# A routing stage with one-hot tiles formed sixteen columns ahead instead of four

## The reference

```python
logits = xf @ gate_w.T                         # 8192 tokens, 8 experts
rw, sel = jax.lax.top_k(logits, 2)
rw = jax.nn.softmax(rw)
for e in range(8):
    we = jnp.sum(jnp.where(sel == e, rw, 0.0), axis=-1)
    h = jax.nn.silu(xf @ w1[e].T) * (xf @ w3[e].T)
    out = out + h @ w2[e].T * we[:, None]
```

## Time and profile before

| | us |
|---|---|
| median of 3 runs (3143.37, 3150.48, 3153.46) | 3150.48 |
| the profiled execution | 3142.74 |
| its span, first to last instruction | 3141.0 |
| routing stage, first DVE operation to last | 2303.93 to 2394.75 |
| expert stage, first instruction to the end | 2396.20 to 3141.0 |

### The profile page before, as it was taken

One profiled execution on the slowest core, in us unless ns is written; L12 is line 12 of the kernel. 1 busy time (PEld: TensorE's weight loads), 2 busy tenths in 40 slices (PEclk: granted clock), 3 DMA queues, 4 the chain that ended last, 5 costly groups with the idle time before them and its releaser, 6 DMA issues. The chain is left out here.

```text
span 3141.0 us, 63979 instructions
## 1 busy us (share of the span) xinstructions
PE 2903.5 (92%) x22889; PEld 1810.8 (58%) x22890; DVE 2306.6 (73%) x4073; ACT 1885.7 (60%) x3422; POOL 655.7 (21%) x940
## 2 busy tenths in 40 slices
PE   5888988886699999999999999998978999999998
PEld 4666766675233333333333333336766888888886
DVE  5776667664799999999999999976876444444443
ACT  3556555652288888888888888883333333333332
POOL 1222122211000000000000000001101555555554
PEclk8889998997699999999999999998879999999999
DMA  1223332332222222222222222216932333333332
GB/s 38 104 91 114 113 115 78 114 113 93 71 87 70 74 80 71 70 68 67 68 65 68 70 71 70 71 42 217 297 123 69 50 50 50 49 49 50 50 49 42
DMA packets 179210, 259.29 MB, mean 83 GB/s; under 512 B 31208, under 2 KB 118528, under 8 KB 179024
## 3 DMA queue, kind: packets, MB, share of 16 engines
q1 hardware_dynamic: 130432, 187.48, 19.2%
q0 software_dynamic: 31152, 52.33, 8.6%
q10 hardware_dynamic: 17440, 16.98, 1.7%
HBM read 134.92 MB, written 119.60 MB: 81 GB/s over the span
## 5 line engine op out<-in xcount | busy, mean ns | idle before, releaser
L868 DVE TENSOR_REDUCE b_mxq<-b_p_m 128x1 f32<-128x1024 f32 x1024 | 1221.9, 1221 | 70.6 <-PE b_p_m L891 63.2
L792 ACT ACTIVATE b_probs<-b_p_e 128x512 f32<-128x512 f32 x2048 | 1105.6, 597 | 147.5 <-PE b_p_e L939 38.7
L891 PE MATMUL b_p_m<-b_kst,b_qst 64*128 64x512 f32 x2048 | 765.0, 454 | 27.7 <-DMA b_vst<-v_d 23.5
L939 PE MATMUL b_p_e<-b_qst,b_kst 64*128 64x512 f32 x2048 | 747.1, 444 | 0.4 <-ACT b_probs L792 0.4
L910 PE MATMUL b_p_o<-b_probs,b_vst 128*32 128x256 f32 x8208 | 642.1, 390 | 0.5 <-ACT b_probs L792 0.4
L939 PEld LDWEIGHTS b_p_e<-b_qst,b_kst 64*128 64x128 f32 x2048 | 315.6, 184 | 419.4 <-ACT b_probs L792 355.0
L1668 ACT ACTIVATE d_act<-d_p_up 128x512 f32<-128x512 f32 x136 | 81.3, 598 | 491.2 <-PE d_p_up L1741 491.2
L910 PEld LDWEIGHTS b_p_o<-b_probs,b_vst 128*32 128x32 f32 x8208 | 168.2, 108 | 324.2 <-issue 187.5
L891 PEld LDWEIGHTS b_p_m<-b_kst,b_qst 64*128 64x128 f32 x2048 | 319.7, 187 | 58.8 <-DVE b_mxq L868 30.9
L1637 POOL DMA_INDIRECT out_dram<-d_y,d_to x136 | 217.7, 1601 | 217.7 <-DVE d_y L1702 205.0
L1756 PE MATMUL d_p_y<-w2T,d_hT 128*128 x1096 | 259.1, 379 | 0.8 <-ACT d_hT L1662 0.8
(11 more groups left out here) (308 smaller groups left out, 4057.7 us busy)
## 6 DMA issues: line engine op xcount, KB each, us to landing
b_qst<-qk_d SPq DMA_DIRECT2D x384, 64.0 KB
b_kst<-qk_d SPq DMA_DIRECT2D x384, 64.0 KB
x1y_d<-a_x1y SPq DMA_DIRECT2D x32, 512.0 KB, 4.4
qk_d<-a_hi SPq DMA_DIRECT2D x32, 512.0 KB, 2.8
qk_d<-a_lo SPq DMA_DIRECT2D x32, 512.0 KB, 3.7
v_d<-a_v_s SPq DMA_DIRECT2D x16, 1024.0 KB, 6.9
b_vst<-v_d SPq DMA_DIRECT2D x64, 256.0 KB
c_xy<-x1y_d SPq DMA_DIRECT2D x16, 1024.0 KB, 8.6
```

Source lines behind the costliest of these rows:

```text
L792: nc.scalar.activation(probs[(2 * step + e % 4 // 2) % BUFS][:, (e % 2) * 512:(e % 2 + 1) * 512], p_e[(slot(e) if more1 else e) % EB][:], ...
L868: V_.reduce_max(mxq[half][:, h, qt:qt + 1], p_m[j % 2][:], AX.X).then_inc(s["m_red"], 1)
L891: mm(p_m[j % 2][:, kh * 512:(kh + 1) * 512], qst[r][rows(h), qt * P:(qt + 1) * P], kst[r][rows(h), kh * 512:(kh + 1) * 512], start=True, s ...
L939: mm(p_e[u % EB][:], kst[r][rows(h), kt * P:(kt + 1) * P], qst[r][rows(h), a * 512:(a + 1) * 512], start=True, stop=True).then_inc(s["e_ps ...
```

## The change

The ring gets 16 places. `is_lo` and `is_hi` become slices of two large tiles, `lo_tiles` and `hi_tiles`, and the integer tables of the prelude (`iota_i`, `val_i`, `slot_i`, `of_i`, `hi_i`, `lo_i`) and `first` are put into places 8 to 15 of them, which the columns reach only after the prelude is done with its tables. `own`, `end_of` and `past` are computed at the end of the prelude, PE multiplies `p_ex` before the columns of expert 0, `experts_of_tiles` moves from e = 2 to e = 1, and the semaphore `rank_ps` goes: one wait on `ex_ps` covers both products.

```diff
+    RING = 16
+    lo_tiles, hi_tiles = sb("lo_tiles", [P, RING, P]), sb("hi_tiles", [P, RING, WIDE])
+    is_lo, is_hi = [lo_tiles[:, r] for r in range(RING)], [hi_tiles[:, r, 0:TILES] for r in range(RING)]
+    spare = [hi_tiles[:, r].bitcast(i32) for r in range(8, 14)]
+    iota_i, iota = spare[0], sb("iota", [P, WIDE])
...
+    first, first_sum = lo_tiles[:, 8:16].rearrange("p r (c e) -> p (r c) e", e=NE), sb("first_sum", [P, C2])
-    RING = 4
-    is_lo = [sb(f"is_lo{r}", [P, P]) for r in range(RING)]
-    is_hi = [sb(f"is_hi{r}", [P, TILES]) for r in range(RING)]
...
         V_.tensor_scalar(other[:], chose[:], -1.0, 1.0, ALU.mult, ALU.add).then_inc(s["other_done"], 1)
+        then(V_.tensor_tensor(own[:], end[:], ident[:, 0:NE], ALU.mult))
+        then(V_.reduce_sum(end_of[:], own[:], AX.X))
+        V_.tensor_scalar(past[:], iota[:, 0:TILES], end_of[:, 0:1], None, ALU.is_ge).then_inc(s["past_done"], 1)
...
-            dve.wait_ge(s["rank_ps"], 1)
+            dve.wait_ge(s["ex_ps"], 1)
...
-            then(V_.tensor_tensor(own[:], end[:], ident[:, 0:NE], ALU.mult))
-            then(V_.reduce_sum(end_of[:], own[:], AX.X))
-            V_.tensor_scalar(past[:], iota[:, 0:TILES], end_of[:, 0:1], None, ALU.is_ge).then_inc(s["past_done"], 1)
...
             if e == 1:
                 ranks()
-            if e == 2:
                 experts_of_tiles()
...
             if e == 0:
                 pe.wait_ge(s["other_done"], 1)
                 mm(p_rank, lower_r[:], other[:], start=True, stop=False, skip_group_check=True)
-                mm(p_rank[:, 1], ones_r[:], other[:, 0], start=False, stop=True, skip_group_check=True).then_inc(s["rank_ps"], 1)
-            if e == 1:
+                mm(p_rank[:, 1], ones_r[:], other[:, 0], start=False, stop=True, skip_group_check=True)
                 pe.wait_ge(s["past_done"], 1)
                 mm(p_ex, ones_b[:], past[0:NE, :], start=True, stop=True).then_inc(s["ex_ps"], 1)
```

More of the change, by code:

```diff
@@ L1356, in invert_places_and_transpose_weights @@
     WIDE = max(P, TILES)
-    iota_i, iota = sb("iota_i", [P, WIDE], i32), sb("iota", [P, WIDE])
+    RING = 16
[3 more added lines that the diff above has]
+    iota_i, iota = spare[0], sb("iota", [P, WIDE])
     lanes_i, early_i, early = sb("lanes_i", [P, TILES], i32), sb("early_i", [P, 2], i32), sb("early", [P, 2])
@@ L1366, in invert_places_and_transpose_weights @@
     valid, empty_i, inv_i, choice_i, before_i = sb("valid", [P, TILES]), sb("empty_i", [P, TILES], i32), sb("inv_i", [P, TILES], i32), sb("choice_i", [P, TILES], i32), sb("before_i", [P, TILES], i32)
-    val_i, val = sb("val_i", [P, C2], i32), sb("val", [P, C2])
+    val_i, val = spare[1][:, 0:C2], sb("val", [P, C2])
     base_i, base = sb("base_i", [P, NE], i32), sb("base", [P, NE])
     total, full, full_i, tiles, end, begin = sb("total", [P, NE]), sb("full", [P, NE]), sb("full_i", [P, NE], i32), sb("tiles", [P, NE]), sb("end", [P, NE]), sb("begin", [P, NE])
-    slot_i, of_i, of, hi_i, lo_i, hi, lo = sb("slot_i", [P, C2], i32), sb("of_i", [P, C2], i32), sb("of", [P, C2]), sb("hi_i", [P, C2], i32), sb("lo_i", [P, C2], i32), sb("hi", [P, C2]), sb("lo", [P, C2])
-    first, first_sum = sb("first", [P, C2, NE]), sb("first_sum", [P, C2])
-    RING = 4
-    is_lo = [sb(f"is_lo{r}", [P, P]) for r in range(RING)]
-    is_hi = [sb(f"is_hi{r}", [P, TILES]) for r in range(RING)]
+    slot_i, of_i, hi_i, lo_i = (spare[r][:, 0:C2] for r in range(2, 6))
+    of, hi, lo = sb("of", [P, C2]), sb("hi", [P, C2]), sb("lo", [P, C2])
+    first, first_sum = lo_tiles[:, 8:16].rearrange("p r (c e) -> p (r c) e", e=NE), sb("first_sum", [P, C2])
     p_s = ctx.enter_context(nc.psum_tensor("r_p_s", [P, 512], f32))
@@ L1378, in invert_places_and_transpose_weights @@
     p_w = [ctx.enter_context(nc.psum_tensor(f"r_p_w{r}", [P, 512], f32)) for r in range(6)]
-    names = ("iotas", "other_done", "rank_ps", "past_done", "ex_ps", "pads", "pad_ps", "ones_done", "n_ps", "dve", "hot", "inv_ps", *(f"raw_in{j}" for j in range(3)), *(f"wT_ps{j}" for j in range(6)), *(f"hi_done{j}" for j in range(4)), *(f"rest_ps{j}" for j in range(4)), *(f"free{j}" for j in range(6)), "less_done")
+    names = ("iotas", "other_done", "past_done", "ex_ps", "pads", "pad_ps", "ones_done", "n_ps", "dve", "hot", "inv_ps", *(f"raw_in{j}" for j in range(3)), *(f"wT_ps{j}" for j in range(6)), *(f"hi_done{j}" for j in range(4)), *(f"rest_ps{j}" for j in range(4)), *(f"free{j}" for j in range(6)), "less_done")
     s = {n: stage_semaphore(nc, ctx, "r_" + n) for n in names}
@@ L1473, in ranks @@
             then(V_.tensor_tensor(lone[:], lone[:], begin[:], ALU.add))
-            then(V_.tensor_tensor(own[:], end[:], ident[:, 0:NE], ALU.mult))
-            then(V_.reduce_sum(end_of[:], own[:], AX.X))
-            V_.tensor_scalar(past[:], iota[:, 0:TILES], end_of[:, 0:1], None, ALU.is_ge).then_inc(s["past_done"], 1)
         def experts_of_tiles():
-            dve.wait_ge(s["ex_ps"], 1)
             then(V_.tensor_copy(ex[:], p_ex))
```

## The result

| | before | after |
|---|---|---|
| median of 6 runs, us | 3149.85 (3143.37 to 3153.46) | 3133.93 (3131.84 to 3138.31) |
| profiled execution, us | 3142.74 | 3137.74 |
| its span, us | 3141.0 | 3136.0 |
| routing stage, first DVE operation to the expert stage's first instruction | 92.3 | 80.1 |
| expert stage, from there to the end | 744.8 | 743.8 |

The ratio of the runs is 0.9955 with a 95% interval of 0.9942 to 0.9969, 0.45% faster. The two profiled executions differ by 5.0 us only: in the one of after the routing stage is 12.2 us shorter and the expert stage 1.0, but the stages ahead of both, which the change doesn't touch, took 8.2 us longer.

A forecast was written before the change was run, and what follows sets the result against it. In the routing stage PE and DVE wait in turns, DVE stalling on a full ring; sixteen places cut turns from 10.12 to 8.03 us, bound by DVE. The gain of 12.1 us gives 3150.5 - 12.1 = 3138.4 us, range 3129 to 3149.

The forecast's parts named there:

- The bound: Routing stage: PE and DVE take turns waiting; DVE stalls on the full ring, seven waits, 11.6 us in all.
- DVE's turn, 8.03 us: Routing stage, per expert: pads 0.72 us plus 16 columns 7.31 us, bounding the turn once the ring is deep enough.
- The forward sum: DVE's times through the routing stage: first column 2313.19, expert 1 done 2330.16, expert 7 done 2379.06 instead of 2391.12.
- No gain in the turn of expert 1, 0.60 us moved ahead of the columns: Routing stage: expert 1 done at 2330.16 against 2330.26; own, end_of and past move earlier, DVE's total unchanged.
- PE's spare time, 0.67 us: Routing stage: PE needs 7.36 us a turn against DVE's 8.03, leaving 0.67 us to spare.
- most to be had: Routing stage, PE-bound turns: six turns shorter by another 0.67 us, 16.1 us gained in all, 3134.4 us.
- The rival of late weights: Routing stage: weight loads landing after 9.6 us make turns 10.65 us and the time 3154 us; chance 0.04.
- The rival of the low clock: Routing stage: PE turns at half clock take 14.7 us, 6.7 more each; four give 3165 us; chance 0.05.
- Depth: Ring in the routing stage: DVE makes 8 columns in the 3.68 us PE takes none; sixteen places are never full.
- The Trainium skill's figure for DVE: Routing stage: about 0.26 us a column, making PE the bound and the gain about 4 us larger; prediction used 0.457.
- the bound of 0.8 us: Start of the expert stage: differing low-clock stretches on PE lose or win at most 0.8 us.
- the forecast 3138.4 us: Whole kernel, median: 3150.5 us less the 12.1 us gained in the routing stage; chance 0.85.

The follow-up runs named there:

- e2: Changed kernel with columns formed only four ahead, the rest of the change kept: ratio to before 1.0002, routing stage 92.6 us.
- e3: Changed kernel with columns formed only six ahead: routing stage 86.7 us, single execution 3145.90 us.
- e5: Changed kernel with columns formed only eight ahead: routing stage 81.6 us, single execution 3132.57 us.
- e4: Changed kernel with is_lo of four columns formed by one DVE operation: 3129.49 us, ratio to before 0.9948, routing stage 74.6 us.
- e7: Changed kernel with six more PE matmuls ahead of the columns in the turns of experts 2 to 6: routing stage 82.8 us, single execution 3141.88 us.
- e8: Changed kernel without the 21 loads of raw weights in the routing stage: routing stage 80.1 us, single execution 3126.55 us.
- e1: The changed kernel run once more, unaltered: 3136.28 us beside 3146.38 for before, ratio 0.9966, routing stage 80.1 us.
- e6: Changed kernel with two more PE matmuls ahead of the columns in the turns of experts 2 to 6: routing stage 80.1 us, single execution 3134.32 us.

## Why the prediction was right, point by point

**The bound.** The prediction read two engines taking turns at waiting, with DVE's stall as the loss. e2, e3 and e5 show it: the order of the change stays, only the depth differs, and the stage's length follows the stall.

**DVE's turn, 8.03 us.** Measured 8.02. The forward sum met the profile within 0.1 us at three places, and the gain of the stage, 12.1 forecast, is 12.2.

**No gain in the turn of expert 1, 0.60 us moved ahead of the columns.** Both as forecast, and e2 gives the small price that the move has in the shallow ring, where the prediction had nothing: 0.3 us. In the deep ring the forward sum comes out without it.

**PE's spare time, 0.67 us.** A term a little too large: the rows gave 7.36 us for PE's turn; e4 measures 7.44, which leaves 0.58, and in e7 0.62 of the added work disappeared. The 0.23 us a column was read from two weight loads of the first columns of a turn. It decided nothing here. The prediction's most to be had, 4.0 us beyond the forecast, was too low: e4 got 5.5. By the starts of PE's turns five turns gave 0.58 each, 2.9 us, and the turns of experts 0, 1 and 7, where I had counted one of the three, another 0.4, 1.1 and 1.2.

**Weights, ACT, the clock.** The loads are hidden, by e8; the rival of late weights falls. For ACT there was no experiment of its own, but in e4's turns, 0.58 us shorter still, PE never waits for it. The rival of the low clock did not occur: from 2327 to 2390 us of the changed kernel the granted clock was 1.00.

**Depth.** The prediction had DVE make eight columns in PE's 3.68 us. e5 shows that eight are just short: 0.2 us of stall is left in a turn. That changed nothing with sixteen.

**The Trainium skill's figure for DVE.** By the Trainium skill's page "VectorE: DVE Perf Modes" (section "The TRN2 errata") a column would have cost DVE about 0.26 us, an estimate from that page, and PE would have been the bound. The turns of 8.02 us, and e4, decide against it: the measured 0.457 holds.

**What follows the stage.** Here the bound of 0.8 us was slightly too narrow. The expert stage took 744.8 us before and 743.8 after, 1.0 less. In both, PE begins it at the lower clock, from 2400.0 to about 2408 before and from 2396.1 to about 2401.1 after, 5.0 us instead of 8.0, which at half speed is up to 1.5 us. e1, of the same kernel as after, rose about 8.2 us behind PE's beginning (2393.5) and took 744.8 again. Granted clock of e1 where PE begins and where it rises:

```profile
2393.00:2394.00 1.00, 0.46 (x2) 0.29 (x2) 0.00 (x0) 0.00 (x0) 0.78 (x1) 0.50 0.38 99
2400.00:2401.00 1.00, 1.00 (x3) 0.72 (x3) 0.96 (x4) 0.12 (x1) 0.00 (x0) 0.50 0.00 0
2401.00:2402.00 1.00, 1.00 (x4) 0.85 (x3) 0.45 (x3) 0.00 (x0) 0.00 (x0) 0.63 0.00 0
```

All ten profiles, whose expert stages have the same code, say the same: where the clock rose 5.0 to 6.1 us behind PE's beginning (after, e4, e2) the expert stage took 743.2 to 743.9 us, where it rose 6.3 to 7.3 us behind (e6, e3, e7) 744.1 to 744.6, and where it rose 7.9 to 8.2 us behind (e5, e8, before, e1) 744.6 to 745.1. So this microsecond goes with the rise of the clock, which differs between two profiles of the same kernel, and is no gain of the change. That the number of matmuls at the lower clock differs between runs of one kernel is what the Trainium skill's page "TensorE: Matmul & The Clock Gate" (Part 1) says, and these runs agree.

**The whole time.** Of the forecast 3138.4 us, 3133.9 was measured, 4.5 us under it. The routing stage gave 0.1 us more than forecast, so nearly all of this comes from elsewhere. Of the six runs only one has a profile (3137.74 us), so this part stays open; over the ten profiles the stages ahead of the routing stage took between 2300.1 and 2313.0 us. The distance from the start to the end of the first of them (to the first maximum of the attention stage) was 806.5 us in the profile of before, 813.6 and 810.7 in the two of the changed kernel, and between 802.5 and 813.0 in the others, though the code is the same in all. Busy time and clock in the first 200 us, of the longest (the changed kernel's first profile) and then of the shortest (e8):

```profile
0.00:100.00 100.00, 58.43 (x539) 45.70 (x541) 55.31 (x103) 36.14 (x55) 19.94 (x25) 0.76 0.13 40
100.00:200.00 100.00, 87.40 (x748) 70.42 (x747) 70.28 (x164) 55.99 (x88) 20.23 (x20) 0.86 0.28 95
```

```profile
0.00:100.00 100.00, 58.02 (x550) 45.45 (x552) 60.04 (x118) 37.77 (x58) 19.92 (x25) 0.84 0.13 40
100.00:200.00 100.00, 87.18 (x782) 70.50 (x780) 69.21 (x158) 59.22 (x94) 20.23 (x20) 0.91 0.31 108
```

The granted clock is 0.76 and 0.86 in the first and 0.84 and 0.91 in the second. That fits a first stage which loses time to the lower clock in varying amounts, but the clock isn't all of it: over the whole of this stretch it was 0.87 in the profile of before and 0.88 in e1, which took 4.2 us longer. The cause of the spread stays open.

## What to carry to other kernels

When two engines hand tiles to each other and one of them also has a block of other work, the depth of the ring has to cover that block, not one tile alone: the block's time over the producer's time for a tile is a first figure, here 3.68 / 0.457 = 8, and it came out just short. Count instead until the first place is released, less the producer's own other work, here 8.6, and take the next whole number. Two lines of waits in opposite directions between the same pair of tiles (PE for DVE 12.4 us, DVE for PE 11.6 us) are the sign of it. Add up each engine's own turn from start-to-start distances in places where it isn't held; the larger one is what the deep ring gave here. In a program whose runs spread by 10 us, the length of the stage in the profile repeats to 0.1 us and tells the experiments apart where the whole time can't.

## What was unexpected of the hardware

An `is_equal` of two broadcast fp32 operands over 4 x 128 elements cost DVE 0.61 us, 0.15 us a tile, less than the 0.20 us of the one-tile `tensor_scalar`, which reads one tensor only. Per element it is 1.2 ns against 1.5 ns: here, taking four at once saved more than the second operand cost.
